# Normalising attention per loaded chunk, guest matmuls at other places, and the order of the value halves

## The reference, cut to what matters

```
h = tok(x)                                             # (4, 3137, 128)
q, k, v = heads(layernorm(h) @ Wq), ... @ Wk, ... @ Wv # 8 heads of 16
attn = softmax(q @ k.T * 16**-0.5 + pos_bias)          # 3137 x 3137 per head
h = h + (attn @ v) @ Wo
n = layernorm(h)
aw = softmax(n @ attn_w + attn_b over tokens); pooled = sum(n * aw)
g = top 2 of softmax(pooled @ gate_w + gate_b), scaled to sum 1
h = h + sum over the 2 experts: g * gelu(gelu(n @ w1 + b1) @ w2 + b2)
```

## Time and profile before

| what | value |
|---|---|
| median of 3 runs (lowest, highest) | 2862.59 us (2859.88, 2864.08) |
| the profiled execution, its own time | 2861.5 us |
| its span, first to last instruction | 2859.8 us |
| PE busy / ACT busy | 2547.9 us (89%) / 2564.2 us (90%) |
| DVE busy / POOL busy | 846.0 us (30%) / 786.6 us (28%) |
| mean granted TensorE clock | 0.986 of full |

### The profile page before, as it was taken

The page is one execution under the profiler, slowest core; times in us unless marked ns, Lnnn a source line. Parts: engine busy times, 40 slices in busy tenths (PEclk is TensorE's granted clock), DMA queues, the critical chain, the costliest instruction groups (busy, mean ns, idle before and its releaser), DMA issues.

```text
span 2859.8 us, 121986 instructions
## 1 busy us (share of the span) xinstructions
PE 2547.9 (89%) x55860; PEld 1222.0 (43%) x55860; DVE 846.0 (30%) x1246; ACT 2564.2 (90%) x2733; POOL 786.6 (28%) x1424
## 2 busy tenths in 40 slices
PE   7988888888889999888899898889999988999997
PEld 3443333333344444433444444334444433455554
DVE  4760111111114233311243343112433421244410
ACT  4769999999999999999999999999999999744553
POOL 2112333333333333333333333332333333100000
PEclk8989999999999999999999999999999999999998
DMA  5550001111111100011111000101110000300010
GB/s 129 176 174 7 29 30 32 32 32 32 33 42 35 35 30 30 30 47 33 42 36 35 30 30 29 49 32 40 35 35 29 29 29 31 127 26 29 15 35 19
DMA packets 65897, 125.31 MB, mean 44 GB/s; under 512 B 10034, under 2 KB 55180, under 8 KB 63892
## 3 DMA queue, kind: packets, MB, share of 16 engines
q1 hardware_dynamic: 63324, 110.93, 12.2%
q0 software_dynamic: 2048, 6.43, 0.6%
HBM read 67.30 MB, written 51.30 MB: 41 GB/s over the span
## 4 chain that ended last, share of the span: by engine, by line
ACT 51%; PE 26%; issue 19%; DMA 2%; DVE 1%; POOL 0%; SPq 0%; ACTq 0%; POOLq 0%
ACT shared L846 50%; PE ps L714 6%; PE ps L722 6%; PE ps L750 5%; PE ps L671 3%; PE ps L668 2%; PE ps L698 1%; DMA k_halves<-halves 1%; PE ps L612 1%; PE ps L606 1%; PE ps L627 0%; DMA band_rows<-band_sb 0%; DVE std L968 0%; POOL ln L915 0%; PE ps L620 0%
## 5 line engine op out<-in xcount | busy, mean ns | idle before, releaser
L846 ACT ACTIVATE shared<-ps 128x1179 f32<-128x1179 f32 x2167 | 2246.4, 1302 | 5.9 <-PE ps L671 4.3
L750 PE MATMUL ps<-shared,va 64*32 64x393 f32 x25600 | 1573.1, 499 | 1.1 <-issue 0.8
L929 POOL TENSOR_TENSOR shared<-shared,e_all 128x310 f32<-128x310 f32 (+19 forms) x1344 | 728.5, 554 | 1539.5 <-ACT shared L846 1533.0
L671 PE MATMUL ps<-qa,ka 48*32 48x393 f16 (+2 forms) x15200 | 728.1, 319 | 149.9 <-ACT shared L846 149.0
L668 PE MATMUL ps<-qa,ka 51*32 51x393 f16 (+8 forms) x13184 | 655.9, 314 | 104.3 <-ACT shared L846 103.8
L750 PEld LDWEIGHTS ps<-shared,va 64*32 64x32 f32 x25600 | 620.3, 139 | 28.9 <-issue 4.5
L671 PEld LDWEIGHTS ps<-qa,ka 48*32 48x32 f16 x15200 | 229.8, 90 | 630.9 <-ACT shared L846 619.7
L668 PEld LDWEIGHTS ps<-qa,ka 51*32 51x32 f16 x13184 | 205.8, 89 | 660.6 <-ACT shared L846 658.7
L1006 DVE COPY xc<-ps 128x393 f32<-128x393 f32 x64 | 36.4, 568 | 1102.6 <-PE ps L750 1102.5
L865 ACT ACTIVATE qa<-ps,b 128x393 f32<-128x393 f32 x256 | 136.4, 585 | 85.0 <-PE ps L714 84.9
L1014 DVE RECIPROCAL sq<-sq 128x393 f32<-128x393 f32 x64 | 167.3, 2615 | 2.2
(11 more groups left out here) (143 smaller groups left out, 1320.7 us busy)
## 6 DMA issues: line engine op xcount, KB each, us to landing
qa<-q_halves SPq DMA_DIRECT2D x64, 196.5 KB
ka<-k_halves SPq DMA_DIRECT2D x64, 196.5 KB
att_rows<-std SPq DMA_DIRECT2D x64, 196.5 KB, 3.4
v_rows<-v_sb SPq DMA_DIRECT2D x4, 1600.0 KB, 6.9
va<-v_rows SPq DMA_DIRECT2D x32, 200.0 KB, 15.9
ln_rows<-ln SPq DMA_DIRECT2D x32, 196.5 KB, 5.6
q_halves<-halves SPq DMA_DIRECT2D x32, 196.5 KB, 3.1
k_halves<-halves SPq DMA_DIRECT2D x32, 196.5 KB, 4.2
```

Of the source, the lines that this page charges most:

```text
L671: last = nc.tensor.matmul(out[x:y, cut:W], ka[r:r + 48, par, k0 + x:k0 + y], qa[r:r + 48, par, q0 + cut:q0 + W], start=True, stop=True, ti ...
L750: last = nc.tensor.matmul(ps[quad:quad + 32, O_PS + half, 0:W], va[r:r + 64, par, :, kt], pr[r:r + 64, g % SLOTS_PR, j], start=(kt == 0), ...
L846: nc.scalar.activation(pr[:, g % SLOTS_PR, 0:m], ps[:, b0:b0 + m, 0:W], ACT.Exp, scale=1.0 / (LIFT * LIFT)).then_inc(s_exp, 1)
L929: nc.gpsimd.tensor_tensor(p, p, e_all[0:keys, n % HEADS, t:t + z - a], ALU.mult).then_inc(s_biased, 1)
```

## The change: what it does, and the diff

1. `drain` keeps only the copy and the add; tick, shuffle, reciprocal and multiply (L1011 to L1017) go. SP stores the sums and denominators as they are, from the buffer that `drain` writes, and `drain` first waits for the store of two passes ago.
2. When an attention chunk is loaded for its Y guest, a second DMA of the same size loads the denominators (`den`). New `normalise(b, c)` on DVE waits for both loads, takes one reciprocal and one multiply of 128 x 393, and raises `s_norm_att`, for which the Y visit now waits. For images 0 to 2 it stands at position 17 of the pass that holds that chunk's Y; for image 3 in the expert stage, at the head of DVE's turn two units before the Y.
3. Chunk 7 is loaded a head later than chunk 6.
4. `guest_plan` replaces `guest_order`: positions 37, 68 and 86 of passes 1 to 13, G in pass 15. Pooling and gate steps move to passes 14 and 15. The late guests follow the same list. With the number of the expert unit U before each:

```diff
+def guest_plan():
+    seen = {"Y": 0, "M": 0, "V": 0, "S": 0}
+    plan = []
+    for p in range(1, 2 * HEADS):
+        y_here = False
+        for pos in (37, 68, 86):
+            if pos == 86:
+                kinds = [("V", "M")]
+            else:
+                kinds = [("S", "V"), ("M", "Y"), ("Y", None)]
+            for kind, after in kinds:
+                c = seen[kind]
+                if c < CH and (after is None or c < seen[after]) and not (kind == "Y" and y_here):
+                    seen[kind] += 1
+                    y_here = y_here or kind == "Y"
+                    plan.append((kind, c, p, pos))
+                    break
+    return plan + [("G", 0, 15, 37)]
...
+    wanted = []
...
-            guest_list = guest_order()
+            guest_list = [(kind, c) for kind, c, p, pos in guest_plan()]
+            chunk_pass = {c: p for kind, c, p, pos in guest_plan() if kind == "Y"}
...
+            late_chunk = {U - 2: guest_list[k % GUESTS][1] for U, k in LATE.items() if guest_list[k % GUESTS][0] == "Y"}
...
-            max_at, pool_exp_at, pool_at = moments(12, 50), moments(12, 85), moments(13, 50)
-            gate_exp_at, pick_at = moments(14, 85), moments(15, 50)
+            max_at, pool_exp_at, pool_at = moments(14, 17), moments(14, 50), moments(15, 17)
+            gate_exp_at, pick_at = moments(15, 60), moments(15, 92)
...
                 def store_half(n, side):
-                    sp.wait_ge(s_norm_o, 2 * n + side + 1)
+                    sp.wait_ge(s_o, at(2 * n + side + 1))
...
                     sp.dma_start(att[:, c % 4], src).then_inc(s_att[c % 4], 16)
+                    src = bass.AP(att_rows, b * (HEADS * head) + c * 32 * W + HD * W, [[head, HEADS], [W, HD], [1, W]])
+                    sp.dma_start(den[c % 4], src).then_inc(s_att[c % 4], 16)
...
                         load_attention(b, 6)
+                    if b >= 0 and into == 3:
                         load_attention(b, 7)
...
-                        pe.wait_ge(s_att[c % 4], 16 * (b * CH // 4 + c // 4 + 1))
+                        pe.wait_ge(s_norm_att, b * CH + c + 1)
...
-                    for half in range(2):
+                    for half in (1, 0) if upper_first and 0 < kt < KT - 1 else (0, 1):
...
+                    for m in turns[g]:
+                        values(m, g < NG and groups[g][-1] % 2 == 0)
...
                 def drain(q):
+                    dve.wait_ge(s_o_out[side], at(16 * (q // 2)))
...
-                    nc.vector.tensor_copy(tick[:, 0:1], o_sb[:, side, 0:1]).then_inc(s_tick, 1)
-                    nc.vector.stream_shuffle(inv[:, side], o_sb[:, side], [HD + i % HD for i in range(32)]).then_inc(s_shuf, 1)
...
-                    nc.vector.reciprocal(inv[:, side], inv[:, side]).then_inc(s_inv, 1)
...
-                    nc.vector.tensor_tensor(o_norm[:, side], o_sb[:, side], inv[:, side], ALU.mult).then_inc(s_norm_o, 1)
+                def normalise(b, c):
+                    dve.wait_ge(s_att[c % 4], 32 * (b * CH // 4 + c // 4 + 1))
+                    nc.vector.reciprocal(den[c % 4], den[c % 4]).then_inc(s_den, 1)
+                    dve.wait_ge(s_den, b * CH + c + 1)
+                    nc.vector.tensor_tensor(att[:, c % 4], att[:, c % 4], den[c % 4], ALU.mult).then_inc(s_norm_att, 1)
...
                 for U in range(1, B * NU + 1):
                     b, c, e = expert_unit(U - 1)
+                    if U in late_chunk:
+                        normalise(B - 1, late_chunk[U])
```

More of the change, by code:

```diff
@@ L81, in score_groups @@
     return groups + tail
[L84 to L91, removed]
+def guest_plan():
[15 more added lines that the diff above has]
+                    break
+    assert len(plan) == 4 * CH and plan[-1][2] <= 13
+    return plan + [("G", 0, 15, 37)]
 def fast_order(B, KT):
@@ L98, in fast_order, with plain @@
     units = [(n, kt, 4 * side + c) for n in range(NBH) for side in range(2) for kt in range(KT) for c in range(4)]
[L99 to L103, removed]
+    plan = guest_plan()
+    places = [(2 * HEADS * (b + 1) + p) * PASS + pos for b in range(B - 1) for kind, c, p, pos in plan]
+    busy = {q // PASS for q in places}
+    wanted = []
+    def plain(u):
+        n, kt, c = units[u]
+        lo = kt * P - REACH
+        return kt < KT - 1 and max(lo, c * (-(-((KT - 1) * P + 65) // CH)), 0) >= min(lo + BAND, (c + 1) * (-(-((KT - 1) * P + 65) // CH)))
+    groups, guest_at, d_at, u = [], {}, {}, 0
     while u < len(units):
@@ L108, in fast_order @@
             size = GMAX - 1
+        elif len(d_at) < len(wanted) and u >= wanted[len(d_at)] and u + 2 < len(units) and plain(u + 2):
+            d_at[len(groups)] = len(d_at)
         groups.append(list(range(u, min(u + size, len(units)))))
@@ L112, in fast_order @@
     batches = [list(range(m, m + 4)) for m in range(0, len(units), 4)]
-    return units, groups, batches, guest_at
+    return units, groups, batches, guest_at, d_at
 def build(nc, B, S, d):
@@ L373, in build @@
             GUESTS = 4 * CH + 1
+            D_STEPS = 7
             EW = 16 * 8
@@ L398, in build @@
             DELAY = 2
-            units, groups, batches, guest_at = fast_order(B, KT)
+            units, groups, batches, guest_at, d_at = fast_order(B, KT)
+            assert T == (KT - 1) * P + 65
             NG = len(groups)
@@ L730, in values @@
                     pe.wait_ge(s_exp, group_of[batches[m][-1]] + 1)
+                    for u in batches[m]:
+                        if u in d_unit:
+                            pe.wait_ge(s_d_exp, d_unit[u] + 1)
                     if any(u in banded_set for u in batches[m]):
@@ L754, in values @@
                     last.then_inc(s_pv, 1)
-                done = 0
-                for g in range(NG + DELAY + AHEAD):
+                for g in range(len(turns)):
                     if g < NG:
                         scores(g)
-                    turn = 1
                     if g in guest_at:
                         visit(guest_at[g], GMAX * (g % 2) + 2)
-                        turn = 0
-                    while done < NB:
-                        lag = g - group_of[batches[done][-1]] - (done % KT == 0)
-                        if lag < DELAY + AHEAD or (turn == 0 and lag < HOLD):
-                            break
-                        values(done)
-                        done += 1
-                        turn = 0
-                while done < NB:
-                    values(done)
-                    done += 1
+                    for m in turns[g]:
+                        values(m, g < NG and groups[g][-1] % 2 == 0)
                 pe.wait_ge(s_exp, NG)
@@ L1115, in _ @@
                 for g in range(NG + 4):
+                    if g in d_at:
+                        exponential(d_at[g])
                     if g in guest_at:
@@ L1119, in _ @@
                         drain(drain_at[g])
+                    if g in normalise_at:
+                        normalise(*normalise_at[g])
                     if g in max_at:
```

83 lines of the change are left out of this document (65 added, 18 removed).

## The result

The kernel after takes 2901.57 us (median of 4 runs, 2898.24 to 2904.04), the one before 2861.24 us beside it (4 runs, 2856.34 to 2864.08). The ratio is 1.0142, with a 95% interval of 1.0124 to 1.016: slower by 40 us. I had forecast 2887 us, with 2880 to 2895 as the range. The sign was right, the size was not: the time lies above the range.

What follows compares the result with a forecast made beforehand. It took ACT's exponentials to bound the attention and PE the expert stage. 2861.5 + 19.7 of waits + 5.1 of clock = 2886.3 us; with the median 1.1 us above the profiled execution, 2887 us, range 2880 to 2895.

Steps and rivals of the forecast that it cites:

- V at position 86: End of attention passes: `rstd` keeps 1.0 us of cover before the drain's copy; 0, up to 5 us without cover.
- the sign of being wrong: The attention moving by over 5 us either way, or PE running through between V and S.
- Order of the late guests: Expert stage: S follows its V by one unit, so PE waits 2.46 us for `rstd` eight times; 19.7 us.
- The clock behind each wait: Expert stage: three of eight waits followed by 1.2 GHz at 1.7 us each; 5.1 us, bounds 0 and 13.6.
- The rule of idle gaps: Skill's warning only of longer gaps, making the clock term 0; kept as rival without clock loss, 2882 us, chance 0.16.
- Start of the experts: First chunk loads and `normalise` are ready before Y0 needs them; 0, up to 4 us with loads several times slower.
- Drains: Attention: four instructions go from each of 64 drains, and the new store wait is already over; 0.
- `normalise` inside the attention: At position 17, 3.2 us for a chunk against 7 us until the earliest Y; 0.
- Half order of the values: Attention: the changed order can bring PE's matmuls forward, but ACT does not wait for PE; 0.
- Number of exponentials: Attention: 99 groups of two and 2067 of three remain, so ACT's own work changes by 0.
- the rival on the faster side, PE setting the pace: Attention: a PE loop sets the exponentials' 1.042 us; 12 ns less each saves 25 us, giving 2857 us; chance 0.04.
- Pooling exponential: Attention: its new mid-pass place, once for each of three images, changes -2.4 to +2.4 us; taken as 0.

Runs made afterwards that it cites:

- experiment 2: Kernel after with the guests of images 0 to 2 at the kernel before's places and order, late guests still in new order: 2887.45 us, ratio 1.0094.
- experiment 4: Kernel after with GpSimd leaving out the band multiplications of key tiles 19 to 24 for chunks 4 to 7: 2886.05 us, ratio 1.0103.
- experiment 5: Kernel after with two rounds in `rstd` in place of three: 2862.05 us, ratio 1.0012.
- experiment 8: Kernel after with three filler matmuls, whose result nobody reads, in front of each late S: 2892.76 us, ratio 1.0114.
- experiment 1: Kernel after with only image 3's late guests in the order of the kernel before, attention places still new: 2873.26 us, ratio 1.0053.
- experiment 6: Kernel after with the lower half of the values always first: 2898.49 us, ratio 1.0138.
- Experiment 3: Kernel after with guests' places and order of the kernel before in both stages; `normalise`, half order, pooling and gate steps stay new: 2859.13 us, ratio 1.0003.

## Why the prediction was right and wrong

*The step that failed: "V at position 86".* I gave it 0, and "tenths of a us for some of 24 passes, up to 5 us" if the cover were gone. The attention grew by 12.7 us, where I had named a change of over 5 us as the sign of being wrong. In experiments 2, 4 and 5 the attention was 10.2, 12.2 and 12.7 us shorter again. These 12.7 us are most of the 14.6 us between 2887 and 2901.6. The working was right for the pass that I looked at: 1.0 us of cover forecast, 1.21 us found. The mistake was to take one pass for all. The earlier trace rows is an even pass. In the kernel before, an odd pass with its V at 80 reads:

```profile
1053.61 1.05 DVE L1063 SCALAR_TENSOR_TENSOR root<-root 128x393 f32<-128x393 f32 x1
1054.70 0.83 DVE L1066 SCALAR_TENSOR_TENSOR ln<-root,ln 128x393 f32<-128x393 f32 x1
1056.49 0.57 DVE L1006 COPY xc<-ps 128x393 f32<-128x393 f32 x1 [0.96 <-PE ps L750]
```

DVE's spare time is 0.96 us, not 3.08, and `rstd` is already stretched. Less 2.1 us for the six positions, that is 1.1 us late: near to what the eight passes show (0.82 us of PE's wait in the one above, 0.68 to 0.92 in all). The rows that I needed stood in the same trace: six V stood at 80 of an odd pass, and their spare time was 0.96, 0.96, 0.69, 0.00, 0.13 and 0.69 us, against 3.08 to 3.25 in the six V at 80 of even passes. Experiments 2, 4 and 5 take the loss away by three different hands: by the place, by GpSimd's work, by the length of `rstd`. The second part of my answer failed too: I wrote that behind the copy PE had two groups of lead, so that a late copy would cost tenths. In the timeline it doesn't: PE stands 0.82 us at L813, the scores queued behind it are late, and ACT waits 1.80 us. I had not priced a fall of the clock in the attention at all; there were two, 3.2 us.

The Trainium skill has the rule that I passed by. "GPSIMD Engine Reference", section "8. Key points", says that GpSimd shares its interfaces to SBUF with VectorE, so that it is in contention with DVE instructions that have two inputs in SBUF. The trace agrees: those of `rstd` with two inputs took 0.57 to 2.12 us. It gives no size for it; the rows do.

*"Order of the late guests": right.* 8 waits, each released by the last instruction of `rstd`, 18.5 us in place of 19.7. I had 2.46 us for one, it was 2.31, and 0.25 us of slower work behind each came on top. (S stood two to five units behind its V in the list before, not two to four as I wrote; the sum doesn't hang on it.)

*"The clock behind each wait": the mechanism right, the size too small.* Five of eight, 8.5 us, in place of three and 5.1. Experiment 8 gives 8.3 us by another way. Against that stand 1.4 us from behind U = 36, so that the stage lost 7.1 us to the clock. The rule of idle gaps in the Trainium skill ("TensorE: Matmul & The Clock Gate", "HAM oscillation — how this bites in real kernels"), by which the term would be 0, doesn't hold here: the waits were 2.3 us. Why five and not the other three, and why experiment 1 had five falls in the attention where the kernel after had two, isn't settled: seven of the eight waits are 2.30 or 2.31 us long, one 2.36. In the kernel after, the three without a fall each come 22.1 us behind the wait before, the others 26 us or more, but that is not the reason. Experiments 2, 4 and 6 have the same eight waits and again five falls each, 20 of 32 in all, and in experiment 4 the third wait, 22.1 us behind the second, is followed by one, while the fifth, seventh and eighth are not (the third wait's row, then its window):

```profile
2561.18 1.68 PE L758 MATMUL ps<-shared,pool_wr 128*128 128x393 f32 x2 [2.30 <-DVE shared L1140]
...
2560.90:2564.30 3.40, 3.12 (x5) 1.84 (x6) 2.17 (x4) 0.00 (x0) 0.54 (x1) 0.51 0.16 59
```

*"Start of the experts": nothing lost, as forecast.* The first `normalise` stood 7.2 us for its load and started 10.8 us after the last exponential (2492.95 - 2482.2). The eight loads were issued in 0.60 to 0.72 us each, forecast 0.68. PE had no idle time of it, and experiment 1 shows the stage no longer than before.

*"Drains", "`normalise` inside the attention", "Half order of the values", "Number of exponentials": nothing, as forecast.* Experiment 3 shows it for all together within about 0.1%, experiment 6 for the half order within about 0.2%. The exponentials without guests keep their pace, 488.50 / 469 = 1.042 us:

```profile
281.70:770.20 488.50, 488.50 (x469) 1.00 0.10 30
```

With that the rival on the faster side, PE setting the pace, is out.

*"Pooling exponential" in the attention: nothing that shows.* PE's three idle times were 2.73, 2.24 and 3.39 us against 2.73, 2.72 and 2.73. One of the three stretches at 1.2 GHz behind them was 6.8 us long, the others 3.4 as before. Experiments 3 and 5 have the new places too, and their attention is 2.0 us longer than before in the one and the same in the other.

As a sum by what was measured: 2861.5 + 18.4 of PE's idle time in the experts + 7.1 of clock + 2.0 of slower work behind the waits + 12.7 for the attention - 0.8 at the start = 2900.9 us, the profiled execution's own time. With the one odd pass above, the same working would have given 1.1 us for each of twelve V, 13 us, and a forecast of about 2900. That this is so near is luck: with all six odd passes it would have been 1.5 us for each on average, 18 us. A late end of `rstd` does not reach the total one for one.

## What to carry to other kernels

Cover worked out from one repetition holds for that repetition. Before a step is moved to the end of a loop's body, look at that end in every kind of body (here odd and even passes), and at what the other engines do there; the shortest spare time counts. A chain of dependent instructions on one engine (here `rstd`, about 7 us) needs more than one turn of the others (5.95 us here) between its start and its consumer, and where that fails on a dense PE, add the clock's price to the wait's.

## What the runs showed of the hardware

- DVE instructions on 128 x 393 float32 with two inputs in SBUF took 0.57 us alone and up to 2.12 us beside GpSimd's elementwise work; not each one beside it was stretched. The reciprocal (2.60 us at 1059.20, beside a GpSimd instruction at 1059.59) and the copy from PSUM (0.55 at 1058.13, in the shown pass) kept their time. L1130 over the whole kernel after (ns: shortest, median, longest):

```profile
L1130 DVE SCALAR_TENSOR_TENSOR root<-root x96: 567/569/2120, 836.6 to 2712.3; 128x393 f32<-128x393 f32 x96
```

- A wait of PE of 2.3 us between dense float32 matmuls was followed by 3.4 us at 1.2 GHz in 5 of 8 cases in each of four kernels; waits of 0.3 to 0.6 us at the same places never were (16 cases). In the attention, where PE also has idle times of 0.5 us around, waits of 0.7 to 0.9 us were followed by it in 2 of 8 cases in the kernel after and in 5 of 8 in experiment 1.
- Each wait of PE in the stage of the experts cost 0.25 us of slower work beside its own length and the clock (table behind experiment 8).
- A float32 matmul of 393 columns is two instructions; 14 of them took 4.62 us from start to the next, 0.33 us each.
